# Attention stage of a transformer block: projections, value turns, reciprocals and weight splits shifted by steps, query waits by head pair

## The chip, the cores and the metric

The kernel runs on one core of a Trainium2 chip. The metric is the device time of one execution, in microseconds (us); lower is better. TensorE (PE) multiplies matrices, VectorE (DVE) and ScalarE (ACT) work elementwise and read its results from PSUM, GpSimd (POOL) works in SBUF, SyncE (SP) issues the DMAs. Each engine goes through a list of its own, and semaphores tie the lists together.

## What is computed

One block on x of shape 2 x 1024 x 512: modulated layer norm, attention, gated residual, modulated layer norm, feed-forward with ternary weights, gated residual. The change lies in the attention: 32 query heads, 8 key/value heads, 64 columns each, causal. Cut to what matters:

```python
h = _layernorm(x) * (1 + ca) + sa
q = (h @ Wq).reshape(b, s, H, D).transpose(0, 2, 1, 3)      # H = 32, D = 64
k = (h @ Wk).reshape(b, s, KVH, D).transpose(0, 2, 1, 3)    # KVH = 8
v = (h @ Wv).reshape(b, s, KVH, D).transpose(0, 2, 1, 3)
q, k = apply_rope(q, pos), apply_rope(k, pos)
k, v = jnp.repeat(k, g, axis=1), jnp.repeat(v, g, axis=1)
scores = jnp.where(causal, q @ k.T / sqrt(D), min)
attn = jax.nn.softmax(scores, axis=-1)
x = x + ga * ((attn @ v).reshape(b, s, H * D) @ Wo)
```

## The kernel before

The program has four stages one after another: `prologue` (norm, transposed input as a high and a low part), `attention`, `project_outputs`, `feed_forward`. Precision is kept by splitting each operand into a high part and a remainder: a copy in ScalarE gives the high part, a subtraction in VectorE or GpSimd the low one.

`attention` goes through eight groups, one for each key/value head with its four query heads. The order of its work is written out by hand. A group is 72 steps; every engine runs the same `step(body, T)` for T = 0 to 71 in its own list (`bodies`, L455 on; group 0 and group 7 are written out, groups 1 to 6 are a loop on each engine, and a run-in of steps 28 to 71 stands ahead of group 0, a run-out of 12 steps behind group 7). What an engine does in a step is fixed by tables:

- Each step has one tile: TensorE turns a 128x128 piece of the exponentials for four heads (`turn`, L651), ScalarE copies the high part (`high`, L695), VectorE makes the low part (`low`, L760), and TensorE multiplies both with the values two steps later (`values`, L663 and L664, `LAG` = 2). `turn(T)` also waits for the low part of T - 2.
- `rows`: a pair of query blocks takes nine steps and has eight score rows (four heads of a large block, then four of a small one), at offsets `ROW_AT` = 0, 1, 3, 4 and 5, 6, 6, 7. A row is `scores` on TensorE (L641 to L643), and one step later `maximum` on VectorE (L768) and `exponentials` on ScalarE (L708). A score writes over PSUM banks that an earlier row must have left (`ROW_FREED`: two rows before for most).
- `X_USES`: the uses of the one PSUM bank for projections, X_BANK: (kind, batch, part, start). A projection (keys and values "kv", or queries of a head pair "qx"/"qy") takes four steps on TensorE (`project`, L599 to L601, a quarter of three matmuls a step, in three steps of four beside a score row). VectorE multiplies by cosine and sine four steps after the start (`rotary_products`, L783, L784), SP swaps halves by DMA a step later (`swap`), GpSimd adds at start + 6 (L822), ScalarE copies the high part at start + 8 (L745 for queries; L741 for keys), GpSimd makes the low part (L833), and SP places both in `q_hl` at start + 10 (`place`). For "kv", ScalarE also copies the values out at start + 4 (L729).
- "v" is the turn of the values through the same bank (`turn_values`, L607), in one step; ScalarE (L734) and VectorE (L795) take the high and the low part one step later. The wait for the bank's earlier user stands at the head of the step (`await_x`).
- `D_AT` = 31 and 66: VectorE makes the reciprocals of the row sums one step ahead (L802), TensorE turns them in the same bank (`turn_den`, L619), ScalarE copies them out (L749).
- `W_HIGH` = 28 and `W_LOW` = 29: the split of the next group's weights, on ScalarE (L715 scales the key columns, L718 the high part) at the head of step 28, on VectorE (L805) at the end of step 29. There is none in group 7.

A use of the bank must find its earlier user gone:

```python
def await_x(g, n):
    uses_done.await_(pe, g, n - 1)
    if X_USES[n - 1][0] == "kv":
        kv_vt.await_(pe, g, KV.index((n - 1) % X_BODY) - (len(KV) if n == 0 else 0))
```

## Time and profile before

| what | value |
|---|---|
| median of 3 runs | 2111.36 us (2105.07 to 2113.36) |
| the profiled execution's own time | 2113.28 us |
| its span, first to last instruction | 2111.5 us |
| busy: PE, DVE, ACT, POOL | 1808.2, 1408.7, 1161.6, 796.9 us |
| mean granted clock of TensorE | 0.946 |
| first and last low part of weights (L805), in the run-in and group 6 | 89.1 and 1112.5 us |

Busy shares are averages over four stages. The distance between one group and the next, seen at L805, is (1112.5 - 89.1) / 7 = 146.2 us. In the timeline a row has the start, the time that the instruction took, and in brackets the engine's idle time before it with what ended it. TensorE's matmuls overlap, so that work is read from start to start; the idle time in brackets goes by a modelled end and comes out somewhat shorter than the gap between starts.

### The profile page before, as it was taken

To read this page: it belongs to the slowest core of one execution; us is meant where nothing else is said; L and a number is where in the kernel's file an instruction comes from. 1 tells how busy PE (TensorE), PEld (TensorE's weight loads), DVE (VectorE), ACT (ScalarE), POOL (GpSimd) and SP (SyncE) were. 2 spreads that over 40 slices of the span, in tenths; PEclk is the share of its full clock that TensorE was granted. 3 is DMA by queue.
4 is the path that set the end of the run, shared out by engine and by line. 5 is a ranking of instruction groups with operands and counts; after the bars stand their busy time and mean duration, and the time that the engine had idled before them with its cause. 6 is when DMAs were issued, how large, how long until landed. Compare 5 with 4: busy or idle time off the path is not lost. (4 is left out here: it accounts for less than half of the span.)

```text
span 2111.5 us, 30964 instructions
## 1 busy us (share of the span) xinstructions
PE 1808.2 (86%) x9601; PEld 1499.0 (71%) x9601; DVE 1408.7 (67%) x1935; ACT 1161.6 (55%) x2283; POOL 796.9 (38%) x532
## 2 busy tenths in 40 slices
PE   4679999999999999999999999357766669999997
PEld 4458878878878887787788888245555547777776
DVE  5347777767767777767777777487797946454543
ACT  1137777767767777677677678343343334232221
POOL 0023333333333333333333332175665714444443
PEclk9789999999999999999999999778888889999999
DMA  6033233233233333323332332667577510101000
GB/s 236 6 79 75 58 98 93 58 86 89 66 77 89 80 74 81 83 73 74 95 78 64 91 73 56 173 168 175 151 184 161 146 55 1 45 1 45 1 26 20
DMA packets 161113, 178.62 MB, mean 85 GB/s; under 512 B 25265, under 2 KB 112057, under 8 KB 160961
## 3 DMA queue, kind: packets, MB, share of 16 engines
q1 hardware_dynamic: 160960, 176.64, 32.9%
q8 instruction: 89, 1.46, 0.3%
q14 instruction: 64, 0.52, 0.1%
HBM read 79.83 MB, written 25.44 MB: 50 GB/s over the span
## 5 line engine op out<-in xcount | busy, mean ns | idle before, releaser
L760 DVE TENSOR_TENSOR p_lo<-ps_b,p_hi 128x512 fp32r<-128x512 f32 x576 | 396.0, 689 | 207.2 <-ACT p_hi L695 203.0
L695 ACT CAST p_hi<-ps_b 128x512 fp32r<-128x512 f32 x576 | 338.4, 587 | 253.2 <-PE ps_b L651 247.4
L768 DVE TENSOR_REDUCE negm<-ps_b 128x1 f32<-128x640 f32 (+7 forms) x512 | 379.6, 751 | 93.6 <-PE ps_b L643 89.7
L708 ACT ACTIVATE p<-ps_b,negm 128x640 f32<-128x640 f32 (+7 forms) x512 | 382.3, 749 | 67.9 <-DVE negm L768 63.3
L651 PE MATMUL ps_b<-ident,p 128*128 128x128 f32 x2304 | 352.8, 276 | 14.4 <-issue 8.7
L641 PE MATMUL ps_b<-k_hh,q_hl 128*128 128x512 f32 (+3 forms) x768 | 267.7, 349 | 16.8 <-DMA q_hl<-rot_x 12.1
L651 PEld LDWEIGHTS ps_b<-ident,p 128*128 128x128 f32 x2304 | 251.3, 141 | 41.4 <-issue 13.8
L663 PE MATMUL ps_b<-p_hi,v_hl 128*128 128x512 f32 x576 | 275.8, 479 | 1.7 <-ACT o_sb L701 1.3
L822 POOL TENSOR_TENSOR rot_c<-rot_c,rot_x 128x512 f32<-128x512 f32 (+1 forms) x96 | 123.3, 1285 | 358.1 <-DMA rot_x<-rot_s 358.1
L642 PE MATMUL ps_b<-k_l,q_hl 128*128 128x512 f32 (+3 forms) x768 | 257.0, 347 | 0.0
L977 PE MATMUL ps_c<-wo_hi,o_hi 128*128 128x512 f32 x256 | 120.4, 470 | 139.3 <-DVE o_lo L1115 139.3
L664 PE MATMUL ps_b<-p_lo,v_hl 128*128 128x512 f32 x576 | 227.9, 396 | 0.0
L817 POOL TENSOR_TENSOR o_sb<-o_sb,o_low 64x512 f32<-64x512 f32 x128 | 163.9, 1283 | 147.1 <-DMA o_low<-o_sb 147.0
L1268 PE MATMUL ps_d<-h_hi,gu 128*128 128x512 f32 x512 | 201.3, 393 | 7.8 <-ACT xn_d L1287 4.6
L1269 PE MATMUL ps_d<-h_lo,gu 128*128 128x512 f32 x512 | 200.0, 391 | 0.0
L599 PE MATMUL ps_b<-hT_hi,w_hi 128*128 128x512 f32 x384 | 157.1, 409 | 38.5 <-DVE w_lo L805 13.2
L641 PEld LDWEIGHTS ps_b<-k_hh,q_hl 128*128 128x128 f32 x768 | 145.1, 189 | 57.9 <-issue 16.9
L977 PEld LDWEIGHTS ps_c<-wo_hi,o_hi 128*128 128x128 f32 x256 | 57.9, 226 | 159.0 <-DVE o_lo L1115 90.4
L642 PEld LDWEIGHTS ps_b<-k_l,q_hl 128*128 128x128 f32 x768 | 145.4, 189 | 28.0
L600 PE MATMUL ps_b<-hT_hi,w_lo 128*128 128x512 f32 x384 | 153.6, 400 | 0.0
L601 PE MATMUL ps_b<-hT_lo,w_hi 128*128 128x512 f32 x384 | 152.2, 396 | 0.0
L1436 DVE TENSOR_TENSOR a<-ps_d,sg 128x512 f32<-128x512 f32 x64 | 44.2, 691 | 158.5 <-PE ps_d L1269 140.8
(141 smaller groups left out, 3420.9 us busy)
## 6 DMA issues: line engine op xcount, KB each, us to landing
rot_x<-rot_s SPq DMA_DIRECT2D x320, 64.0 KB, 2.0
q_hl<-rot_s SPq DMA_DIRECT2D x128, 128.0 KB, 2.3
q_hl<-rot_x SPq DMA_DIRECT2D x128, 128.0 KB, 2.4
o_low<-o_sb SPq DMA_DIRECT2D x128, 128.0 KB, 2.2
attention_out<-o_sb SPq DMA_DIRECT2D x128, 128.0 KB, 2.5
o_raw<-attention_out SPq DMA_DIRECT2D x32, 512.0 KB, 4.9
rd<-attention_out SPq DMA_DIRECT2D x64, 256.0 KB, 9.0
wf<-in_L_ffn_w_gate_up SPq DMA_DIRECT2D x16, 512.0 KB, 11.6
```

Source lines behind the costliest of these rows:

```text
L641: pe.matmul(ps[:, bank, 0:n], q, k_hh[:, unit, k0:k0 + n], start=True, stop=False)
L642: ins = pe.matmul(ps[:, bank, 0:n], q, k_l0[:, unit, k0:k0 + n], start=False, stop=(k0 + n < nk))
L651: ins = pe.transpose(ps[:, T_BANK + T % 2, h * P:(h + 1) * P], p_32[:, parity, h, column * P:(column + 1) * P], ident[:])
L663: pe.matmul(ps[:, O_BANK, :], v_hl[:, unit, j, :], p_hi[:, T % P_RING, :], start=(j == 0), stop=False)
L664: pe.matmul(ps[:, O_BANK, :], v_hl[:, unit, j, :], p_lo[:, T % P_RING, :], start=False, stop=(j == i)).then_inc(pv_done, 1)
L695: act.copy(p_hi[:, T % P_RING, :], ps[:, T_BANK + T % 2, :]).then_inc(phi_ready, 1)
L708: act.activation(p_32[:, parity, h, column * P:column * P + nk], s, ACT.Exp, bias=negm[:, k:k + 1], scale=1.0, accum_out=den[:, unit, h, i ...
L760: dve.tensor_tensor(p_lo[:, T % P_RING, :], ps[:, T_BANK + T % 2, :], p_hi[:, T % P_RING, :].bitcast(F32), ALU.subtract).then_inc(plo_read ...
L768: dve.tensor_reduce(negm[:, k:k + 1], s, AX.X, ALU.max, negate=True).then_inc(max_ready, 1)
L977: pe.matmul(ps[:, i, t, :], hi, wo_hi[:, kk, :], start=(kk == 0), stop=False)
L1268: pe.matmul(ps[:, bank + half, :], gu[:, m, half, k, :], h_hi[:, parity, k, :], start=(k == 0), stop=False)
L1269: i = pe.matmul(ps[:, bank + half, :], gu[:, m, half, k, :], h_lo[:, parity, k, :], start=False, stop=(k == CT - 1))
```

## The change

Four things. In `X_USES` the four query projections of batch 1 start one step later (9, 14, 19, 24 become 10, 15, 20, 25), with all that hangs on them by an offset, on every engine and in SP's queue; the turn of batch 0's values starts one step earlier (44 becomes 43), with its copies. The weight split moves one step later on both engines (28, 29 become 29, 30). The reciprocals move one step earlier on VectorE, to two steps ahead of their turn. And TensorE's wait for placed queries, which stood ahead of the first row of a block for both head pairs, is divided: ahead of row 0 for the first pair, and ahead of row 2, the first to read the second pair's heads, for the second.

```diff
--- before.py
+++ after.py
@@ -290,15 +290,15 @@
 RB = PAIRS * len(ROWS)
 ROWS_BEFORE = 8
 
-X_USES = [("kv", 1, 1, 1), ("v", 1, 0, 7), ("qx", 1, 0, 9), ("qx", 1, 1, 14), ("qy", 1, 0, 19), ("qy", 1, 1, 24),
-          ("kv", 0, 0, 33), ("kv", 0, 1, 38), ("v", 0, 0, 44), ("qx", 0, 0, 46), ("qx", 0, 1, 51), ("qy", 0, 0, 56),
+X_USES = [("kv", 1, 1, 1), ("v", 1, 0, 7), ("qx", 1, 0, 10), ("qx", 1, 1, 15), ("qy", 1, 0, 20), ("qy", 1, 1, 25),
+          ("kv", 0, 0, 33), ("kv", 0, 1, 38), ("v", 0, 0, 43), ("qx", 0, 0, 46), ("qx", 0, 1, 51), ("qy", 0, 0, 56),
           ("qy", 0, 1, 61), ("kv", 1, 0, 68)]
 X_HERE = 6
 LAST_ROW = {("qx", 0): 39, ("qy", 0): 55, ("qx", 1): 7, ("qy", 1): 23}
 X_BODY = len(X_USES)
 D_AT = [31, 66]
 START = 28
-W_HIGH, W_LOW, W_LOAD = 28, 29, 2
+W_HIGH, W_LOW, W_LOAD = 29, 30, 2
 
 
 class Events:
@@ -622,16 +622,17 @@
                 unit, _, i, h, _, k = row_of(r)
                 first = (r // 8 + 1) % 4
                 if k == 0 and first == 0:
-                    for n in ([7, 9, 10] if unit == 0 else [0, 2, 3]):
-                        if X_USES[n][0] == "kv":
-                            kv_lo.await_(pe, g, KV.index(n))
-                            kv_hi.await_(pe, g, KV.index(n))
-                        else:
-                            q_place[buf_of(n)].await_(pe, g, QBUF[buf_of(n)].index(n))
-                if k == 0 and first == 2:
-                    for n in ([11, 12] if unit == 0 else [4, 5]):
-                        buf = buf_of(n)
-                        q_place[buf].await_(pe, g, QBUF[buf].index(n) - (len(QBUF[buf]) if unit == 0 else 0))
+                    n = 7 if unit == 0 else 0
+                    kv_lo.await_(pe, g, KV.index(n))
+                    kv_hi.await_(pe, g, KV.index(n))
+                if k in (0, 2) and first == 0:
+                    n = (9 if unit == 0 else 2) + h // 2
+                    buf = buf_of(n)
+                    q_place[buf].await_(pe, g, QBUF[buf].index(n))
+                if k in (0, 2) and first == 2:
+                    n = (11 if unit == 0 else 4) + h // 2
+                    buf = buf_of(n)
+                    q_place[buf].await_(pe, g, QBUF[buf].index(n) - (len(QBUF[buf]) if unit == 0 else 0))
                 rows_p.await_(pe, g, r - ROW_FREED[k])
                 nk = (i + 1) * P
                 q = q_hl[:, h, i * P:(i + 1) * P]
@@ -796,7 +797,7 @@
                                       v_hl[:, unit, :, 0:D].bitcast(F32), ALU.subtract).then_inc(x_used, 1)
                 for g, t in body.tile(T, 0):
                     low(g, t)
-                for g, d in body.dens(T, -1):
+                for g, d in body.dens(T, -2):
                     rows_p.await_(dve, g, 23 if d == 0 else 55)
                     dens_turned.await_(dve, g, d - 1)
                     dve.reciprocal(rd[:], den[:, d].rearrange("p h i -> p (h i)")).then_inc(rd_ready, 1)
```

In the changed kernel, lines behind the waits are numbered one higher (L805 is L806). Where the program moves, in the loop of groups 1 to 6; rows that only set registers and wait for nothing are left out.

VectorE, steps 28 to 31, before (b_whi_ready is the high weights' semaphore, b_phi_ready that of a tile's high part, b_s_ready that of a score row):

```order
L783 TENSOR_TENSOR rot_c<-ps_b,cos 128x512 [waits b_x_ready]
L784 TENSOR_TENSOR rot_s<-ps_b,sin 128x512
L768 TENSOR_REDUCE negm<-ps_b 128x1 [waits b_s_ready]
L760 TENSOR_TENSOR p_lo<-ps_b,p_hi 128x512 [waits b_phi_ready]
L768 TENSOR_REDUCE negm<-ps_b 128x1 [waits b_s_ready]
L760 TENSOR_TENSOR p_lo<-ps_b,p_hi 128x512 [waits b_phi_ready]
L805 TENSOR_TENSOR w_lo<-w_raw,w_hi 128x1536 [waits b_whi_ready]
L760 TENSOR_TENSOR p_lo<-ps_b,p_hi 128x512 [waits b_phi_ready]
L802 RECIPROCAL rd_b<-den 128x32 [waits b_rd_turned,b_p_ready]
L768 TENSOR_REDUCE negm<-ps_b 128x1 [waits b_s_ready]
```

and now:

```order
L784 TENSOR_TENSOR rot_c<-ps_b,cos 128x512 [waits b_x_ready]
L785 TENSOR_TENSOR rot_s<-ps_b,sin 128x512
L769 TENSOR_REDUCE negm<-ps_b 128x1 [waits b_s_ready]
L761 TENSOR_TENSOR p_lo<-ps_b,p_hi 128x512 [waits b_phi_ready]
L803 RECIPROCAL rd_b<-den 128x32 [waits b_rd_turned,b_p_ready]
L761 TENSOR_TENSOR p_lo<-ps_b,p_hi 128x512 [waits b_phi_ready]
L806 TENSOR_TENSOR w_lo<-w_raw,w_hi 128x1536 [waits b_whi_ready]
L769 TENSOR_REDUCE negm<-ps_b 128x1 [waits b_s_ready]
L761 TENSOR_TENSOR p_lo<-ps_b,p_hi 128x512 [waits b_phi_ready]
```

The rotation (cosine, sine) stands behind step 28's low part and not ahead of its maximum; the reciprocal has come forward by one low part; the low part of the weights stands behind step 30's low part and directly ahead of a maximum.

ScalarE, steps 27 to 30, before (rot_s is a query copy, b_t_ready the turn's semaphore):

```order
L745 CAST rot_s<-rot_c 128x512 [waits b_rotated0]
L715 ACTIVATE w_raw<-w_raw 128x4x64 [waits b_w_in]
L316 REGISTER_ALU [waits b_k_scaled]
L718 CAST w_hi<-w_raw 128x1536 [waits b_x_ready]
L695 CAST p_hi<-ps_b 128x512 [waits b_pv_done,b_t_ready]
L701 COPY o_sb<-ps_b 128x512 [waits b_o_out1,b_pv_done]
L708 ACTIVATE p,den<-ps_b,negm 128x1024 [waits b_max_ready]
L695 CAST p_hi<-ps_b 128x512 [waits b_pv_done,b_t_ready]
```

and now:

```order
L696 CAST p_hi<-ps_b 128x512 [waits b_pv_done,b_t_ready]
L702 COPY o_sb<-ps_b 128x512 [waits b_o_out1,b_pv_done]
L709 ACTIVATE p,den<-ps_b,negm 128x1024 [waits b_max_ready]
L746 CAST rot_s<-rot_c 128x512 [waits b_rotated0]
L716 ACTIVATE w_raw<-w_raw 128x4x64 [waits b_w_in]
L316 REGISTER_ALU [waits b_k_scaled]
L719 CAST w_hi<-w_raw 128x1536 [waits b_x_ready]
L696 CAST p_hi<-ps_b 128x512 [waits b_pv_done,b_t_ready]
L709 ACTIVATE p,den<-ps_b,negm 128x1024 [waits b_max_ready]
```

The query copy, the scaling and the high weights stand behind a high copy, an output copy and an exponential row that they stood ahead of.

TensorE, steps 43 and 44, before (b_x_used and b_vt_ready are the semaphores of the bank's earlier user):

```order
L663 MATMUL ps_b<-p_hi,v_hl 128x512 [waits b_plo_ready]
L664 MATMUL ps_b<-p_lo,v_hl 128x512
L641 MATMUL ps_b<-k_hh,q_hl 128x256 [waits b_p_ready]
L642 MATMUL ps_b<-k_l,q_hl 128x256
L643 MATMUL ps_b<-ident_r,mask_r 128x128
L316 REGISTER_ALU [waits b_x_used]
L316 REGISTER_ALU [waits b_p_ready,b_vt_ready]
L651 MATMUL ps_b<-ident,p 128x128 [waits b_plo_ready]
L651 MATMUL ps_b<-ident,p 128x128 x3
L663 MATMUL ps_b<-p_hi,v_hl 128x512 [waits b_plo_ready]
L664 MATMUL ps_b<-p_lo,v_hl 128x512
L607 MATMUL ps_b<-ident,rot_c 128x64 x8
```

and now:

```order
L316 REGISTER_ALU [waits b_x_used]
L316 REGISTER_ALU [waits b_vt_ready]
L652 MATMUL ps_b<-ident,p 128x128 [waits b_plo_ready]
L652 MATMUL ps_b<-ident,p 128x128 x3
L664 MATMUL ps_b<-p_hi,v_hl 128x512 [waits b_plo_ready]
L665 MATMUL ps_b<-p_lo,v_hl 128x512
L607 MATMUL ps_b<-ident,rot_c 128x64 x8
L642 MATMUL ps_b<-k_hh,q_hl 128x256 [waits b_p_ready]
L643 MATMUL ps_b<-k_l,q_hl 128x256
L644 MATMUL ps_b<-ident_r,mask_r 128x128
L316 REGISTER_ALU [waits b_p_ready]
L652 MATMUL ps_b<-ident,p 128x128 [waits b_plo_ready]
```

The wait for b_x_used and b_vt_ready now stands ahead of step 43's turn, and the value turn (L607) ahead of step 43's score.

## Rows read from the trace of the kernel before

**Rows 1.** The page's part on engines: busy us (share of the span) xinstructions

```profile
PE 1808.2 (86%) x9601; PEld 1499.0 (71%) x9601; DVE 1408.7 (67%) x1935; ACT 1161.6 (55%) x2283; POOL 796.9 (38%) x532
```

**Rows 2.** Who waited for whom, TensorE: us in total, times, longest

```profile
PE ps_b L619 <- DVE rd_b L802: 13.9, 15, 1.3
...
PE ps_b L641 <- DMA q_hl<-rot_x: 12.1, 8, 2.8
PE ps_b L599 <- DVE v_hl L795: 11.1, 16, 1.4
```

**Rows 3.** Timeline, group 3, steps 8 to 10, VectorE then TensorE

```profile
615.90 1.28 DVE L760 TENSOR_TENSOR p_lo<-ps_b,p_hi 128x512 fp32r<-128x512 f32 x2
...
616.04 0.50 PE L599 MATMUL ps_b<-hT_hi,w_hi 128*128 128x512 f32 x1 [0.97 <-DVE v_hl L795]
...
617.60 0.61 PE L651 MATMUL ps_b<-ident,p 128*128 128x128 f32 x4
```

**Rows 4.** Timeline, group 3, steps 27 to 32: TensorE, ScalarE, VectorE

```profile
652.76 0.40 PE L599 MATMUL ps_b<-hT_hi,w_hi 128*128 128x512 f32 x1
...
653.46 0.40 PE L641 MATMUL ps_b<-k_hh,q_hl 128*128 128x512 f32 x1
...
654.43 0.60 PE L651 MATMUL ps_b<-ident,p 128*128 128x128 f32 x4
...
663.68 0.33 PE L641 MATMUL ps_b<-k_hh,q_hl 128*128 128x128 f32 x1
...
652.98 0.62 ACT L745 CAST rot_s<-rot_c 128x512 fp32r<-128x512 f32 x1
...
655.41 0.58 ACT L695 CAST p_hi<-ps_b 128x512 fp32r<-128x512 f32 x1
...
657.46 0.60 ACT L695 CAST p_hi<-ps_b 128x512 fp32r<-128x512 f32 x1
...
659.03 1.31 ACT L695 CAST p_hi<-ps_b 128x512 fp32r<-128x512 f32 x2
662.42 1.12 ACT L708 ACTIVATE p<-ps_b,negm 128x1024 f32<-128x1024 f32 x1 [2.09 <-DVE negm L768]
...
658.09 0.69 DVE L760 TENSOR_TENSOR p_lo<-ps_b,p_hi 128x512 fp32r<-128x512 f32 x1 [0.23 <-ACT p_hi L695]
...
661.22 1.16 DVE L768 TENSOR_REDUCE negm<-ps_b 128x1 f32<-128x1024 f32 x1
```

**Rows 5.** Timeline, group 3, steps 43 to 46: TensorE, ScalarE, VectorE

```profile
685.14 0.62 PE L651 MATMUL ps_b<-ident,p 128*128 128x128 f32 x4
...
687.09 0.65 PE L651 MATMUL ps_b<-ident,p 128*128 128x128 f32 x4 [0.56 <-ACT rot_c L729]
...
691.86 0.50 PE L599 MATMUL ps_b<-hT_hi,w_hi 128*128 128x512 f32 x1 [0.28 <-DVE v_hl L795]
...
686.38 0.58 ACT L729 COPY rot_c<-ps_b 64x512 f32<-64x512 f32 x1
...
691.12 0.69 DVE L795 TENSOR_TENSOR v_hl<-ps_b,v_hl 128x512 fp32r<-128x512 f32 x1 [1.42 <-ACT v_hl L734]
```

**Rows 6.** Timeline, group 3, steps 63 to 68: TensorE, then ScalarE

```profile
728.22 0.49 PE L641 MATMUL ps_b<-k_hh,q_hl 128*128 128x512 f32 x1 [1.10 <-DMA q_hl<-rot_x]
...
739.31 0.22 PE L641 MATMUL ps_b<-k_hh,q_hl 128*128 128x128 f32 x1
...
733.69 1.11 ACT L708 ACTIVATE p<-ps_b,negm 128x1024 f32<-128x1024 f32 x1 [0.57 <-DVE negm L768]
...
737.30 1.12 ACT L708 ACTIVATE p<-ps_b,negm 128x1024 f32<-128x1024 f32 x1 [0.23 <-DVE negm L768]
```

**Rows 7.** Timeline and one stretch (busy by engine, then PEclk): group starts, group 6

```profile
595.03 1.05 PE L651 MATMUL ps_b<-ident,p 128*128 128x128 f32 x4 [1.86 <-issue]
...
595.14:598.55 3.41, 3.41 (x13) 3.03 (x14) 0.69 (x1) 1.17 (x2) 0.34 (x1) 0.50 0.45 112
...
1182.98 0.49 PE L641 MATMUL ps_b<-k_hh,q_hl 128*128 128x512 f32 x1 [2.12 <-DMA q_hl<-rot_x]
```

## The prediction

> **What bounds the kernel now.** The share of busy time comes first: TensorE 86%, VectorE 67%, ScalarE 55% [rows 1]. The change touches only the attention stage, so the next view is who TensorE waits for. Of its waits there, three kinds belong to instructions that the change moves: 13.9 us for the reciprocals, 12.1 us for placed queries (the longest, 2.8 us, in the run-in before the first group), 11.1 us for split values [rows 2]. That is 37.1 us, under 2% of the time. For the rest of the stage TensorE's queue is the clock: eight groups of 72 steps. Then I read the timeline of one ordinary group (group 3 of 0 to 7) around each moved instruction, on TensorE, ScalarE and VectorE side by side. Each of these works strictly through its own list, so the question at every place is not who is late now, but what stands next in line when a stall goes. Times below are starts unless I say otherwise; I sum against the profiled execution (span 2111.5, own time 2113.28 us) and carry the difference over to the median of 2111.36.
>
> **Query projections of batch 1 one step later (9 to 10, and so on).** At step 9 TensorE stands still until the values' low half is made, and projects at 616.04 [rows 3]. With the projection at step 10, that wait is covered by step 9's scores. But the same VectorE queue makes step 8's low part after the low values, at 615.90, for 0.69 us, so until 616.65 with the signal; and TensorE's turn of step 10 must have it. Before, that turn stood at 617.60 with a projection quarter of about 0.70 us (652.76 to 653.46) done that is now still to do [rows 3, 4]. Gain: 617.60 - 616.65 - 0.70 = 0.25 us a group, not the 1 us of the stall: 8 x 0.25 = -2.0 us. The later multiplications on VectorE, copies on ScalarE and GpSimd, and the swap and place DMAs of SP all move by the same step; their readers stand five steps or more behind, so no queue there gets late.
>
> **Steps 27 to 32: the weight split and the first reciprocal.** This is the largest term. ScalarE has 2.43 us of work (query copy 652.98, then key scaling and high weights, until 655.41) which now comes one step later [rows 4]. Before, it sat where ScalarE had nothing else; step 28's high copy followed at 655.41 and step 29's at 657.46, 2.05 us on. Now step 28's high copy comes first. The turn that it reads stands at 654.43 before; the projection quarter of step 24 has moved behind it, so it comes 0.70 earlier, at 653.73, and the copy some 0.64 later, 654.37. Then the 2.05 us, and then the 2.43 us: step 29's high copy is at 654.37 + 2.05 + 2.43 = 658.85, 1.39 later than before. VectorE's low part of step 29 follows by 0.63, at 659.48 against 658.09 [rows 4]. From there to the maximum of the third wide row VectorE has 3.13 us of work in both orders (661.22 - 658.09: two low parts, low weights, reciprocal). But the low weights now stand behind step 30's low part, which waits for ScalarE: high copy 30 at 658.85 + 1.57 = 660.42, so 661.05 for the low part, while VectorE is free at 660.35. That adds 0.70. The maximum comes at 661.22 + 1.39 + 0.70 = 663.31. Exponential (1.20 on) and the score that waits for it (1.26 on) follow: 665.77 against 663.68 [rows 4]. The stall on the reciprocal goes entirely, and is already inside this difference: TensorE waits for the exponential in its place. That is 2.09; with a few hundredths for each signal that has no row of its own I take **+2.2 us for the seven groups** that split weights, +15.4 us. Bounds: 0, if ScalarE drains faster than its rows say, to 2.5 (x7 = 17.5). The last group has no split: 0.
>
> **Value turn one step earlier (44 to 43).** The wait for the previous projection's user stands at the head of the step. ScalarE's copy of the values starts at 686.38, and TensorE resumes at 687.09 [rows 5]. That copy depends on nothing in step 43, so its time stays; TensorE now stops at 685.14 and not after step 43. The stall grows from 0.72 (1.95 less 1.23 us of work in step 43) to 1.95. In return the 0.45 us before the projection at 691.86 (0.28 by the ends of the matmuls) is covered: +0.78 net if nothing else is late. Something is: the low values (691.12) now stand ahead of step 44's low part, as at step 8, and TensorE's turn 46 needs that part. ScalarE reaches the high values at about the same time as before, so that part ends at 691.12 + 0.60 + 0.69 = 692.41, the turn is at 692.48 instead of 690.49, and the projection 0.92 later at 693.40: +1.54. I take **+1.5 x 7 = +10.5 us**, with +0.8 and +1.6 as ends, since the low part's place in the queue is fixed by the order.
>
> **Waits divided by head pair, second reciprocal.** At step 63 the first score waits for a placement that only the third one, at step 66, reads. This goes: 1.26 us here (728.22; 1.10 in the row by the ends), 9.3 us by ends over the seven groups, 10.4 us by starts [rows 2, 6]. At step 66 the stall on the reciprocal goes too, but the chain VectorE to ScalarE to VectorE takes over: with the reciprocal at step 64, ahead of the rotation, the exponential of 733.69 comes 1.26 - 0.26 = 1.00 earlier, and so does that at 737.30; the score that needs it comes 1.26 us after, at 737.56 against 739.31. So 1.75 us where the placement stall was 1.26: 0.5 more. Sum: 10.4 + 7 x 0.5 = **-13.9 us**. In the run-in the 2.8 us stall goes [rows 2]: -2.8 us. The waits at steps 9, 27 and 45 do not bind now.
>
> **Clock.** The new idle times, 1.95 us at step 43 and some 2.4 us at step 32, are as long as some at the group's start. One of those, 1.86 us, was followed by a stretch granted 0.50, that is 1.2 GHz instead of 2.4 [rows 7]; it cost that group some 1.6 us (half of 3.4). I allow one or two such stretches, +2 us; the bounds are 0 and all fourteen new idle times, +22 us.
>
> Sum: -2.0 + 15.4 + 10.5 - 13.9 - 2.8 + 2 = **+9 us**: 2120 on the median. Half a percent, 10.6 us, is about what can be told from no change here: faster is under 2101, slower over 2122.
>
> **A rule against this.** TensorE has the highest occupancy [rows 1], and VectorE and ScalarE have a third or more of their time free. The Trainium skill (Perfetto Trace Analysis, section Identifying the Most-Contended Engine) says that the engine with the highest occupancy is the one to optimise first. By that rule work shifted on the other two is free and the stalls taken from TensorE are the result: the first rival. The rows of steps 28 to 30, where ScalarE and VectorE have next to no gaps, speak against it.
>
> **Rivals.** (1) *All three kinds of stall vanish and nothing else is late*: -37.1 us, 2074. For it: each stall has a named releaser that the change moves away. Against: at steps 8 and 29 the next instruction in the same queues is read by TensorE within two steps. Chance 0.08. (2) *The pile-up at 28 to 32 does not cost*, because ScalarE and VectorE recover before TensorE needs the third wide row, and the turn at 43 costs only 0.8: -2.0 + 0 + 5.6 - 13.9 - 2.8 = -13, 2098. It needs ScalarE to gain 2 us in three steps in which it has no gap. Chance 0.15. (3) *Slower, by the clock*: the long new idles are followed by the 1.2 GHz level in most groups. Each costs 1.6 us; with seven or more of the fourteen it is +7 + 11 to +22, 2129 to 2140, so 2134. It decides from about three stretches on. For it: 1.86 us was enough once. Against: the stall before 1182.98 in another group, which was longer, was not followed by it; the matmul after it took 0.49 us, as at 728.22 [rows 6, 7]. Chance 0.20. (4) Forecast: 2120, its own range 2112 to 2128, chance 0.57.
>
> **Range and chances.** 2098 to 2135 leaves out rival 1, half of rival 2 and the upper part of rival 3, under 0.2. Faster: rival 1 and two thirds of rival 2, 0.18. Slower: rival 3 and the upper part of the forecast's range, 0.42. Same: 0.40. The forecast lies just under the bound.
>
> **What would show it.** In the profile after: TensorE's wait for split values before the projection gone, and waits for low parts (turn 10, turn 31, turn 46) in its place; no wait for reciprocals in groups with a split, but a wait for the exponential of about 2.5 us at step 32; the wait for the value copy about 1.9 instead of 0.6 us; no wait for placed queries; a wait for an exponential near step 68. A wait for the low parts that stays under 0.3 us at turns 31 and 46 would refute the two large terms; the count of stretches at 0.50 settles the clock.

## The result, and the profile after

The changed kernel takes 2136.36 us (median of 6 runs, 2132.55 to 2149.44) where the kernel before takes 2110.86 us beside it (6 runs, 2105.07 to 2113.57): a ratio of **1.0133, 95% interval 1.0102 to 1.0163**. It is slower by 25.5 us. The forecast was 2120, its range 2098 to 2135: the sign of the sum was right, its size was not, and the time lies just above the range.

The profiled execution had its own time of 2149.44 us, a span of 2147.6 us and a mean granted clock of 0.936. It is the longest of the six. A second profiled execution of the same kernel (below) had a span of 2134.5; where one number might depend on the execution I give both.

The page's part on engines, after (the line that answers to [rows 1]): busy us (share of the span) xinstructions.

```profile
PE 1838.7 (86%) x9601; PEld 1529.7 (71%) x9601; DVE 1409.6 (66%) x1935; ACT 1158.0 (54%) x2283; POOL 791.6 (37%) x532
```

The number of instructions is the same on each engine. VectorE, ScalarE and GpSimd are busy for the same time within 6 us; TensorE is busy 30.5 us longer (1838.7 against 1808.2) with the same 9601 matmuls. More busy time for equal work is the first sign that the clock has a part in this.

Who waited for whom on TensorE, after: us in total, times, longest. It answers to [rows 2].

```profile
PE ps_b L642 <- ACT p L709: 28.8, 27, 3.3
PE ps_b L652 <- DVE p_lo L761: 16.7, 20, 1.0
...
PE ps_b L652 <- issue: 12.5, 6, 2.4
PE ps_b L652 <- ACT rot_c L730: 10.6, 6, 1.8
```

Of the rows of the attention stage, scores that wait for an exponential (L642, L709), turns that wait for a low part (L652, L761), and turns of step 43, which now stand behind the value turn's wait for the copy of the values (L730), have grown most. The reciprocal and the placed queries, 13.9 and 12.1 us in [rows 2], have no row left, and the wait for split values (11.1 us there) has shrunk to 1.4 us, once. So nearly 36 us of stalls that the change was to remove are gone, and three rows have 56 us of waits where the kernel before had 9 us in them (4.3, 0.9 and 3.9).

A table by stretches of a group says where the time went. Each number is the time from the turn (matmul L651, after L652) of one step to that of another, from starts in the timeline of TensorE. "Before" is group 3; "after" is group 3 of the first execution, which happened to have no stretch at 1.2 GHz at steps 31 to 48; the last column is what the other groups of that execution showed.

| steps of a group | before | after, group 3 | after, other groups with the split |
|---|---|---|---|
| 9 to 14 | 11.62 | 11.38 | 11.37 to 11.39 |
| 14 to 27 | 26.25 | 25.62 | 25.62 |
| 27 to 33 | 12.21 | 15.62 | 15.46 to 15.88 |
| 33 to 36 | 5.98 | 5.77 | 7.34 to 8.36 |
| 38 to 43 | 10.87 | 12.77 | 12.77 to 12.84 |
| 43 to 48 | 9.89 | 9.69 | 9.66 to 9.69, or 11.71 to 11.73 |
| 63 to 69 | 14.23 (mean of seven 14.44) | 12.39 | 12.38 to 12.39 |

**Steps 27 to 32.** Timeline, after, group 3: ScalarE, VectorE, GpSimd, TensorE. It answers to [rows 4].

```profile
670.31 0.59 ACT L696 CAST p_hi<-ps_b 128x512 fp32r<-128x512 f32 x1 [1.80 <-PE ps_b L652]
...
672.38 0.63 ACT L746 CAST rot_s<-rot_c 128x512 fp32r<-128x512 f32 x1
...
673.43 1.48 ACT L719 CAST w_hi<-w_raw 128x1536 fp32r<-128x1536 f32 x1
674.81 0.58 ACT L696 CAST p_hi<-ps_b 128x512 fp32r<-128x512 f32 x1
...
681.07 1.11 ACT L709 ACTIVATE p<-ps_b,negm 128x1024 f32<-128x1024 f32 x1 [3.61 <-DVE negm L769]
...
675.42 0.69 DVE L761 TENSOR_TENSOR p_lo<-ps_b,p_hi 128x512 fp32r<-128x512 f32 x1 [1.40 <-ACT p_hi L696]
...
677.00 0.69 DVE L761 TENSOR_TENSOR p_lo<-ps_b,p_hi 128x512 fp32r<-128x512 f32 x1 [0.63 <-ACT p_hi L696]
677.61 2.29 DVE L806 TENSOR_TENSOR w_lo<-w_raw,w_hi 128x1536 fp32r<-128x1536 f32 x1
679.82 1.21 DVE L769 TENSOR_REDUCE negm<-ps_b 128x1 f32<-128x1024 f32 x1
...
676.99 1.30 POOL L823 TENSOR_TENSOR rot_c<-rot_c,rot_x 128x512 f32<-128x512 f32 x1 [1.30 <-DMA rot_x<-rot_s]
...
676.16 0.66 PE L652 MATMUL ps_b<-ident,p 128*128 128x128 f32 x4 [0.94 <-DVE p_lo L761]
...
682.32 0.33 PE L642 MATMUL ps_b<-k_hh,q_hl 128*128 128x128 f32 x1 [3.03 <-ACT p L709]
```

Read it from the top: step 28's high copy (670.31), then the query copy and the high weights, and only then step 29's high copy at 674.81. VectorE's low part of step 29 follows at 675.42. The low weights (L806, 677.61) stand behind step 30's low part, and the maximum that the exponential needs comes at 679.82, the exponential at 681.07, the score at 682.32. This is the predicted chain, link for link. One link has another length: the low weights take 2.29 us; in the kernel before they take 1.75 (the experiments below say why). The score stood still for 3.03 us, where I had said about 2.5.

**Steps 43 to 46.** Timeline, after, group 3: ScalarE, VectorE, TensorE. It answers to [rows 5].

```profile
704.80 0.58 ACT L730 COPY rot_c<-ps_b 64x512 f32<-64x512 f32 x1
...
709.82 0.69 DVE L796 TENSOR_TENSOR v_hl<-ps_b,v_hl 128x512 fp32r<-128x512 f32 x1 [1.59 <-ACT v_hl L735]
710.42 1.28 DVE L761 TENSOR_TENSOR p_lo<-ps_b,p_hi 128x512 fp32r<-128x512 f32 x2
...
705.51 0.65 PE L652 MATMUL ps_b<-ident,p 128*128 128x128 f32 x4 [1.77 <-ACT rot_c L730]
...
711.16 0.66 PE L652 MATMUL ps_b<-ident,p 128*128 128x128 f32 x4 [0.82 <-DVE p_lo L761]
...
712.12 0.39 PE L599 MATMUL ps_b<-hT_hi,w_hi 128*128 128x512 f32 x1
```

The turn of step 43 stands idle for 1.77 us by the ends of the matmuls (0.56 in [rows 5]), because the value turn's wait is now at the head of that step. The projection at 712.12 waits for nothing; in its place the turn of step 46, at 711.16, waits 0.82 us for a low part that is behind the low values.

**Steps 63 to 68.** Timeline, after, group 3: TensorE and ScalarE. It answers to [rows 6].

```profile
757.53 0.33 PE L642 MATMUL ps_b<-k_hh,q_hl 128*128 128x128 f32 x1 [0.27 <-ACT p L709]
...
752.70 1.12 ACT L709 ACTIVATE p<-ps_b,negm 128x1024 f32<-128x1024 f32 x1 [0.77 <-DVE negm L769]
...
756.27 1.11 ACT L709 ACTIVATE p<-ps_b,negm 128x1024 f32<-128x1024 f32 x1 [1.27 <-DVE negm L769]
```

The score follows its exponential (756.27) after 1.26 us, as predicted, and is idle for only 0.27 us.

**The clock.** Timeline of TensorE, after, group 2, at steps 32 and 43, and then busy time by engine in four stretches (us, PE busy (x), PEld busy (x), DVE, ACT and POOL busy (x), PEclk, DMA share, GB/s). The first three windows follow step 43 of group 2, step 32 of group 2 and step 32 of group 4; the last one follows step 43 of group 3.

```profile
525.60 0.33 PE L642 MATMUL ps_b<-k_hh,q_hl 128*128 128x128 f32 x1 [2.99 <-ACT p L709]
...
550.37 0.65 PE L652 MATMUL ps_b<-ident,p 128*128 128x128 f32 x4 [1.77 <-ACT rot_c L730]
```

```profile
551.00:557.80 6.80, 6.80 (x29) 5.34 (x28) 2.77 (x5) 4.21 (x11) 1.04 (x1) 0.50 0.00 1
527.10:530.50 3.40, 3.40 (x14) 3.04 (x14) 1.27 (x3) 2.19 (x8) 1.27 (x1) 0.50 0.19 42
837.70:841.10 3.40, 3.40 (x13) 2.92 (x12) 1.58 (x3) 3.04 (x7) 0.16 (x1) 0.50 0.05 10
...
705.50:712.30 6.80, 5.97 (x41) 5.00 (x42) 3.79 (x7) 4.46 (x12) 1.28 (x1) 1.00 0.06 14
```

After the idle of 2.99 us at step 32 and after that of 1.77 us at step 43 there are 3.4 and 6.8 us at a granted clock of 0.50, the 1.2 GHz level. In 6.8 us at 0.50 TensorE did 29 matmuls, at 1.00 it did 41. In the seven groups with a split, ten of the fourteen places are followed by such a stretch: step 32 in groups 0, 1, 2, 4, 5 and 6, step 43 in groups 1, 2, 5 and 6. A stretch after step 32 makes steps 33 to 36 take 7.35 us instead of 5.77, one after step 43 makes steps 43 to 48 take 11.7 instead of 9.69. In all: 6 x 1.58, and 1.0 more in group 1, whose stretch is longer (6.8 us), is 10.5; 4 x 2.02 is 8.1; together **18.6 us**. (The 6.8 us behind step 43 cost less than half their length; the 0.82 us that the turn of step 46 waits in group 3 is not there in these groups, so a part of the slow work falls into that wait.)

The account of the attention stage, from its first to its last matmul (1234.0 us before, 1265.6 after, by these profiled executions):

| term | predicted | found in the trace | from |
|---|---|---|---|
| query projections, step 9 to 14 | -2.0 | -1.9 | 8 x (11.38 - 11.62) |
| steps 14 to 36 without the clock | +15.4 | +18.0 | 7 x (47.01 - 44.44), group 3 |
| value turn, steps 38 to 48 without the clock | +10.5 | +11.9 | 7 x (22.46 - 20.76) |
| waits divided and second reciprocal, 63 to 69 | -13.9 | -14.4 | 7 x (12.39 - 14.44) |
| run-in to the first group | -2.8 | -2.9 | 51.79 against 54.70 |
| clock | +2 | +18.6 | the paragraph above |
| sum | +9 | +29.3 | measured +31.5; the loop's head (step 69 to 0) has most of the rest, 2.1 |

### The profile page after: what moved, and what is told of

It reads as the page before. It is cut to its first block and busy times, and to the rows that moved or that the text cites. A ratio compares the mean times of both kernels' runs of the same rounds, so it can differ in the third digit from the quotient of the medians.

```text
span 2147.6 us, 30941 instructions
## 1 busy us (share of the span) xinstructions
PE 1838.7 (86%) x9601; PEld 1529.7 (71%) x9601; DVE 1409.6 (66%) x1935; ACT 1158.0 (54%) x2283; POOL 791.6 (37%) x532
## 5 line engine op out<-in xcount | busy, mean ns | idle before, releaser
L761 DVE TENSOR_TENSOR p_lo<-ps_b,p_hi 128x512 fp32r<-128x512 f32 x576 | 395.1, 688 | 227.2 <-ACT p_hi L696 222.4
L709 ACT ACTIVATE p<-ps_b,negm 128x640 f32<-128x640 f32 (+7 forms) x512 | 382.6, 750 | 76.5 <-DVE negm L769 72.1
L652 PE MATMUL ps_b<-ident,p 128*128 128x128 f32 x2304 | 360.2, 280 | 40.8 <-DVE p_lo L761 16.7
L652 PEld LDWEIGHTS ps_b<-ident,p 128*128 128x128 f32 x2304 | 256.5, 143 | 72.9 <-DVE p_lo L761 32.9
L642 PE MATMUL ps_b<-k_hh,q_hl 128*128 128x512 f32 (+3 forms) x768 | 270.6, 352 | 29.0 <-ACT p L709 28.8
L664 PE MATMUL ps_b<-p_hi,v_hl 128*128 128x512 f32 x576 | 280.3, 487 | 1.1 <-ACT o_sb L702 0.6
L823 POOL TENSOR_TENSOR rot_c<-rot_c,rot_x 128x512 f32<-128x512 f32 (+1 forms) x96 | 123.5, 1286 | 393.3 <-DMA rot_x<-rot_s 393.3
L642 PEld LDWEIGHTS ps_b<-k_hh,q_hl 128*128 128x128 f32 x768 | 148.0, 193 | 71.6 <-ACT p L709 37.0
L599 PE MATMUL ps_b<-hT_hi,w_hi 128*128 128x512 f32 x384 | 156.6, 408 | 28.7 <-DVE w_lo L806 13.2
L601 PE MATMUL ps_b<-hT_lo,w_hi 128*128 128x512 f32 x384 | 153.4, 399 | 0.0
```

The source lines that it names most:

```text
L642: pe.matmul(ps[:, bank, 0:n], q, k_hh[:, unit, k0:k0 + n], start=True, stop=False)
L652: ins = pe.transpose(ps[:, T_BANK + T % 2, h * P:(h + 1) * P], p_32[:, parity, h, column * P:(column + 1) * P], ident[:])
L664: pe.matmul(ps[:, O_BANK, :], v_hl[:, unit, j, :], p_hi[:, T % P_RING, :], start=(j == 0), stop=False)
L709: act.activation(p_32[:, parity, h, column * P:column * P + nk], s, ACT.Exp, bias=negm[:, k:k + 1], scale=1.0, accum_out=den[:, unit, h, i ...
L761: dve.tensor_tensor(p_lo[:, T % P_RING, :], ps[:, T_BANK + T % 2, :], p_hi[:, T % P_RING, :].bitcast(F32), ALU.subtract).then_inc(plo_read ...
```

## The experiments

All differences below are edits of the kernel before or of the changed kernel. The kernel before ran beside each of them: 2113.31 us (23 runs) beside the waits alone, the value turn alone, projections with split, and the useless work; 2112.78 (7 runs) beside the query projections alone, the sum that waits, the waits with reciprocals, and the low weights in two parts; 2113.94 (10 runs) beside the other three. Each ratio is to these.

### The three parts of the change, one by one

**The waits alone**, on the kernel before:

```diff
-                    for n in ([7, 9, 10] if unit == 0 else [0, 2, 3]):
...
+                if k in (0, 2) and first == 0:
+                    n = (9 if unit == 0 else 2) + h // 2
+                    buf = buf_of(n)
+                    q_place[buf].await_(pe, g, QBUF[buf].index(n))
```

> The kernel before with the waits for queries divided by head pair, and nothing else. Queue theory: the stall ahead of step 63's first score goes in seven groups (10.4 us by starts) and in the run-in (2.8 us); the reciprocal still stands behind step 65's low part, so the chain VectorE to ScalarE moves by just the stall and nothing comes on top: 2111 - 13 = 2098 us. Rival: the placement is merely awaited three steps later, at step 66, and the stall reappears there: 2111 us, with a wait for placed queries of about 1 us ahead of the third row. Clock: no new idle time, so no more stretches at 0.50 in the attention stage than the two of before.

Measured: 2097.34 us (9 runs, 2090.95 to 2107.71), ratio 0.9919 (0.9893 to 0.9944). The wait for placed queries has no row any more, so the rival (the stall comes back at step 66) is refuted, and steps 63 to 69 take 12.88 us (12.77 in group 0). This part gains 16 us by itself. I had priced it at 10.4 and 2.8, that is 13.2; the ratio's interval, 12 to 23 us, holds that.

**The value turn alone** at step 43, on the kernel before:

```diff
-          ("kv", 0, 0, 33), ("kv", 0, 1, 38), ("v", 0, 0, 44), ("qx", 0, 0, 46), ("qx", 0, 1, 51), ("qy", 0, 0, 56),
+          ("kv", 0, 0, 33), ("kv", 0, 1, 38), ("v", 0, 0, 43), ("qx", 0, 0, 46), ("qx", 0, 1, 51), ("qy", 0, 0, 56),
```

> The kernel before with the turn of batch 0's values at step 43 instead of 44, and nothing else. Queue theory: the wait for the value copy grows from 0.6 to about 1.8 us, the wait ahead of step 46's projection goes and one for step 44's low part takes its place: 1.7 us for each of seven groups, +12 us. Clock theory: the idle time is followed by a stretch at 0.50 in about four of the seven groups, 2 us each, +8 us: 2131 us. Without the clock's part: 2123 us. If the loss seen in the changed kernel came only because it was late from step 33 already: no change, 2111 us.

Measured: 2132.05 us (9 runs, 2129.67 to 2148.61), ratio 1.0084 (1.0057 to 1.0111). Steps 38 to 43 take 12.78 to 12.86 us in the groups with a split (10.87 before); the wait L651 for the copy is 10.6 us, 6 times, longest 1.8, just as in the changed kernel. Three of the seven groups (2, 4 and 6) have a stretch at 0.50 after it. The median is where I had expected it (2131), but not all of it for the reason that I gave: these stretches cost 3.9 us by steps 43 to 48 (10.53, 11.70 and 10.76 instead of 9.67 to 9.69), not 8. Another 4.8 us lie at steps 63 to 69, where two groups (1 and 2) have a stretch at 0.50 behind the wait for placed queries; that wait is 1.3 to 2.1 us in groups 1 to 6. So half of the clock's share was hit by luck.

**Query projections and weight split together**, without the divided waits and with the old reciprocal:

```diff
-X_USES = [("kv", 1, 1, 1), ("v", 1, 0, 7), ("qx", 1, 0, 9), ("qx", 1, 1, 14), ("qy", 1, 0, 19), ("qy", 1, 1, 24),
+X_USES = [("kv", 1, 1, 1), ("v", 1, 0, 7), ("qx", 1, 0, 10), ("qx", 1, 1, 15), ("qy", 1, 0, 20), ("qy", 1, 1, 25),
...
-W_HIGH, W_LOW, W_LOAD = 28, 29, 2
+W_HIGH, W_LOW, W_LOAD = 29, 30, 2
```

> The kernel before with the four query projections one step later and the weight split at steps 29 and 30, and nothing else (reciprocals at their old place). Queue theory: 0.24 us gained at step 9 in eight groups, some 2.7 us lost from step 27 to step 33 in seven, because the high weights stand ahead of step 29's high copy and the low weights behind step 30's low part: +17 us. Clock theory on top: the idle time at step 32 is followed by a stretch granted 0.50 in most groups, 1.4 to 1.6 us each, +9 us: 2137 us together. If the clock has nothing to do with it: 2128 us and no stretches at 0.50 after step 32. Rival (the low weights are slowed by the GpSimd sum beside them, not by their place in the queue): the low weights take 2.1 us or more here too, and the rest of the loss is small.

Measured: 2141.55 us (4 runs, 2139.43 to 2155.91), ratio 1.0138 (1.0087 to 1.0189). Steps 27 to 33 take 16.6 to 17.4 us, over one more than in the changed kernel. The waits of TensorE say why (us in total, times, longest):

```profile
PE ps_b L641 <- DMA q_hl<-rot_x: 22.1, 16, 2.8
PE ps_b L641 <- ACT p L708: 17.5, 18, 2.0
```

The wait for placed queries comes 16 times instead of 8 [rows 2]. The scores of step 27 wait for the first two query projections of batch 1, one for each head pair, at once. The second of them now starts at step 15 and is placed at step 25, which is late for step 27: the score stands still for 0.92 us in group 3 (at 660.91), and the row has grown by 10 us for eight groups. The prediction said that the waits at step 27 do not bind; that holds in the kernel before, and it holds in the changed kernel only because that one has divided them. So two parts of the change lean on each other here. The 2137 us that I had expected did not have this wait. The rival, low weights slowed to 2.1 us or more by GpSimd's sum, is refuted as the cause of this loss: they take 1.86 to 1.92 us here. The idle time at step 32 is 1.8 to 2.0 us, and in four of the seven groups (1, 3, 5 and 6) a stretch at 0.50 follows it.

Added up by ratios, the three parts give -0.81 + 0.84 + 1.38 = +1.41%, and the whole is +1.33%. That is agreement within the intervals only (0.3, 0.3 and 0.5), which together leave room for over 10 us. By the attention stages of the profiled executions the three give -13.5 + 21.5 + 30.3 = +38 us and the whole +31.5 (+29.7 in its second execution): the 10 us of waits at step 27 are counted in the parts and do not exist in the whole.

**Query projections alone**, the split left at steps 28 and 29 (only the first of the two edits above):

> The kernel before with the four query projections one step later, and nothing else: the weight split stays at steps 28 and 29. ScalarE then waits at the head of step 28 for a projection that TensorE makes in that step. Queue theory, worked out from the rows of the kernel before: step 29's high copy comes about 2.1 us later than before, the third wide maximum about 2.5 us later; less than with the split moved as well (4.2 to 4.6 us there, with the reciprocal at its old place). So 2111 - 2 + 17 = 2126 us, and up to 8 us more where stretches at 0.50 follow: 2126 to 2134. Rival (the split has to move with the projections, and its own move costs nothing): the same as with both moved, 2141 us, or slower.

Measured: 2158.13 us (4 runs, 2149.89 to 2162.54), ratio 1.0206 (1.0174 to 1.0239). This expectation (2126 to 2134) was wrong in direction: I had thought that the split, left where it was, would cost less. It costs some 15 us more than both together; the rival, the same as with both moved or slower, is what came. Some of the 15 us are the clock's: all seven groups have a stretch at 0.50 at steps 31 to 32, where the run with both has four. Timeline, group 3: ScalarE, VectorE, GpSimd, TensorE.

```profile
664.75 0.42 ACT L715 ACTIVATE w_raw<-w_raw 128x256 f32<-128x256 f32 x1
669.39 1.48 ACT L718 CAST w_hi<-w_raw 128x1536 fp32r<-128x1536 f32 x1 [4.22 <-PE ps_b L601]
670.77 0.57 ACT L695 CAST p_hi<-ps_b 128x512 fp32r<-128x512 f32 x1
...
674.91 2.83 DVE L805 TENSOR_TENSOR w_lo<-w_raw,w_hi 128x1536 fp32r<-128x1536 f32 x1
...
674.85 1.28 POOL L817 TENSOR_TENSOR o_sb<-o_sb,o_low 64x512 f32<-64x512 f32 x1
677.23 1.64 POOL L822 TENSOR_TENSOR rot_c<-rot_c,rot_x 128x512 f32<-128x512 f32 x1 [1.10 <-DMA rot_x<-rot_s]
...
678.73 0.28 PE L619 MATMUL ps_b<-ident,rd_b 128*32 128x128 f32 x1 [2.56 <-DVE rd_b L802]
```

The new high weights overwrite those that the last query projection still reads. They stand at the head of step 28 in ScalarE's list, and that projection now ends in the same step: they wait 4.22 us for its last matmul (L601), and step 28's high copy (670.77) stands behind them. Moving the split along by a step was therefore the better choice once the projections had moved. The 18 us of steps 14 to 36 in the changed kernel are thus a price of moving the projections with the split behind them, which lands where ScalarE and VectorE are already late. What the split costs when it moves alone was not measured.

### The low weights of 2.1 to 2.6 us

In the changed kernel the low weights took 2.20, 2.14, 2.25, 2.29, 2.14, 2.29 and 2.58 us in groups 0 to 6, beside GpSimd's sum (L823) for 0.58, 0.53, 0.63, 0.68, 0.52, 0.68 and 0.96 us. In the kernel before, beside nothing, they took 1.75 in every group. In the timeline of steps 27 to 32 above the sum starts at 676.99 and ends at 678.29, the low weights at 677.61. So GpSimd's sum was made to wait for them:

```diff
                     buf_swap[buf].await_(pool, g, BUF[buf].index(n))
+                    if n == X_HERE - 1 and body.holds(0, 0, KVH - 2):
+                        splits_lo.await_(pool, g, 0)
```

> The changed kernel, in which GpSimd's sum for the last query projection of batch 1 waits until the low weights are made (seven groups), so that the two do not lie side by side. In the changed kernel the low weights take 2.14 to 2.58 us where a sum of GpSimd overlaps them, 1.75 in the kernel before where none does. Theory (VectorE's operation with two inputs in SBUF waits for GpSimd's): the low weights are back at 1.75 us, the score at step 32 stands 0.4 to 0.8 us earlier, some 3.5 us in all and a little more if a stretch at 0.50 goes: 2132 us against the 2136 of the changed kernel. Rival: the low weights are slower because of something else at that place (ScalarE's copies, DMAs): 2.1 us or more as before, and no gain.

Measured: 2132.15 us (4 runs, 2128.0 to 2137.69), ratio 1.0087 (1.0059 to 1.0114). Timeline of VectorE and GpSimd, group 3:

```profile
668.05 1.75 DVE L806 TENSOR_TENSOR w_lo<-w_raw,w_hi 128x1536 fp32r<-128x1536 f32 x1
...
669.88 1.26 POOL L825 TENSOR_TENSOR rot_c<-rot_c,rot_x 128x512 f32<-128x512 f32 x1 [3.75 <-DVE w_lo L806]
```

With nothing beside them they take 1.75 us again, in all groups, and steps 27 to 33 take 15.01 to 15.09 us instead of 15.46 to 15.88: 7 x 0.56 = 3.9 us by the trace. The median is 4.2 us lower; by the ratios it is more (0.46%, 9.7 us), but eight stretches at 0.50 follow the two steps instead of ten (groups 2, 3, 5 and 6 at both), so I take the trace's 4 us as the size. The rival, something else at that place, is refuted. This is the part by which the second term was too small: 18.0 - 4.0 = 14.0 against the 15.4 predicted.

Each overlap lengthens the low weights by nearly the whole overlap (0.54 us for 0.68, in the run with the query projections alone 1.08 for 1.22), and there the operation of GpSimd that began *while* the low weights ran (677.23) took 1.64 us instead of 1.28. The one that comes second is held up. The run with useless work below has both cases as well: in groups 2 to 5 GpSimd's sum begins 0.07 to 0.24 us behind the low weights, which take 1.75 us, and the sum takes 2.65 to 2.83 us instead of 1.29; in groups 1 and 6 it begins ahead of them, and they take 2.84 and 2.78 us. The Trainium skill (SBUF — State Buffer, section Who interferes with whom) says that a VectorE instruction with two inputs in SBUF contends with a GpSimd instruction that reads SBUF, and that the issue order decides who blocks; the trace agrees both ways round.

### The clock, with useless work in the idle time

In every group with a split, TensorE does 16 useless transposes ahead of the value turn's wait at step 43 and 8 useless matmuls ahead of the late score of step 32. The results of the kernel are the same; the work is extra.

```diff
+            def fill_turns(g, T):
...
+                for _ in range(4):
+                    for h in range(GQ):
+                        pe.transpose(ps[:, T_BANK + T % 2, h * P:(h + 1) * P],
+                                     p_32[:, parity, h, column * P:(column + 1) * P], ident[:])
+            def fill_bank(g):
+                for _ in range(8):
+                    pe.matmul(ps[:, O_BANK, :], k_l0[D:P, 1, 0:P], k_hh[D:P, 1, 0:512], start=False, stop=False)
```

> The changed kernel with useless matmuls put into TensorE's two new idle times: 16 transposes ahead of the wait at step 43 (a bank that the next turn writes over) and 8 matmuls with zeros ahead of the score at step 32. They take 1.4 and 1.9 us of idle times of 1.95 and about 2.9 us. Clock theory: TensorE now does more work and ends earlier, since the stretches at 0.50 after steps 32 and 43 (10 in the profile of the changed kernel) do not come: some 18 us less than the profiled run of the changed kernel, 8 to 12 us less than its median of 2136, so 2124 to 2128 us. Queue theory alone (the clock follows something else): the fillings lie in idle time and cost nothing, 2136 us, and as many stretches at 0.50 as without them.

Measured: 2130.45 us (10 runs, 2118.86 to 2134.76), ratio 1.0063 (1.0038 to 1.0088), span 2117.1. That is over the 2124 to 2128 expected and under the 2136 of the rival; the count of stretches decides between them. Timeline of TensorE in group 2 at step 43, then at step 32, and the stretch behind step 43 that answers to the one from 551.00 above:

```profile
535.35 1.93 PE L661 MATMUL ps_b<-ident,p 128*128 128x128 f32 x16
537.21 0.66 PE L652 MATMUL ps_b<-ident,p 128*128 128x128 f32 x4
```

```profile
511.54 2.10 PE L666 MATMUL ps_b<-k_hh,k_l 64*128 64x512 f32 x8
514.10 0.33 PE L642 MATMUL ps_b<-k_hh,q_hl 128*128 128x128 f32 x1 [0.46 <-ACT p L726]
```

```profile
537.20:544.00 6.80, 5.97 (x42) 5.00 (x42) 3.88 (x7) 4.47 (x12) 1.27 (x1) 1.00 0.06 14
```

The kernel with more work is the faster one. Steps 38 to 43 last nearly as long as before the filling (12.70 us, before 12.8), so nothing of the stall itself is won; but no stretch at 0.50 follows step 43 in any group and only one follows step 32 (group 1), and outside that group steps 33 to 36 take 5.77 us, and 43 to 48 take 9.66 to 9.70 in all. The attention stage is 19.5 us shorter than in the first execution of the changed kernel and 17.7 shorter than in the second. (Not all of that is the clock: in groups 2 to 5 the low weights begin ahead of GpSimd's sum and take 1.75 us, which is 2 us in all; in groups 1 and 6 they take longer, and steps 27 to 33 with them, so that 1 us is left.) By the times the gain is smaller: 8.4 us by the differences to the kernel before beside each (17.1 against 25.5), 15 by the ratios. The profiled execution was the fastest of its ten, so others may have had more such stretches than it. The clock term is thus 8 to 18 us, on any count several times the 2 that I had put.

The Trainium skill (TensorE: Matmul & The Clock Gate, section What's actually happening) says that the lower level is the default and that activity releases it. The trace agrees: ten stretches at 0.50 without the useless matmuls, one with them.

### The same kernel again, and the value turn back in its place

**Again**, unaltered:

> The changed kernel, unaltered, for a second profiled execution. In the first one ten stretches at a granted clock of 0.50 followed the new idle times (six after step 32, four after step 43), and that execution was 13 us above the kernel's own median. If the clock term is made by those stretches, a second execution near the median should have fewer or shorter of them: about 10.4 + 8.1 - 13 = some 5 to 6 us instead of 18.5 in the groups, that is three to five of the fourteen places, and steps 27 to 33 and 38 to 43 unchanged within 0.1 us (15.46 to 15.88, 12.8). If instead the stretches are a fixed part of this order of work, ten again, and the spread between executions lies outside the attention stage. Median 2136 either way.

Measured: 2138.26 us (4 runs, 2132.0 to 2147.09), ratio 1.0128 (1.0091 to 1.0165); the profiled execution has a span of 2134.5. I had expected three to five stretches after steps 32 and 43 in it. There are ten, as in the first one, at other places: step 32 in groups 0, 1, 2, 3, 4 and 6, step 43 in groups 1, 2, 3 and 4. Two of them:

```profile
543.00:549.80 6.80, 6.80 (x30) 5.54 (x29) 2.04 (x4) 3.62 (x10) 1.27 (x1) 0.50 0.02 4
519.10:522.50 3.40, 3.40 (x14) 3.02 (x13) 1.67 (x5) 2.41 (x7) 0.91 (x1) 0.51 0.19 43
```

The attention stage is nearly as long (1263.7 against 1265.6 us), so the rival that I had named holds: ten of fourteen belong to this order of work, and 11 of the 13 us between the two executions lie elsewhere. The turn of step 0 in group 0 starts at 146.17 us in the first execution and at 138.49 in the second: 7.7 of the 13.1 us have come together before the first group begins, and 7.0 of them before the attention stage's first matmul (94.4 against 87.3 us), in a part of the program that the change does not touch. The executions of the other kernels fall on 138 to 147 us at this place as well, the kernel before on 145.73. The cause is open.

**The changed kernel with the value turn back at step 44:**

```diff
-          ("kv", 0, 0, 33), ("kv", 0, 1, 38), ("v", 0, 0, 43), ("qx", 0, 0, 46), ("qx", 0, 1, 51), ("qy", 0, 0, 56),
+          ("kv", 0, 0, 33), ("kv", 0, 1, 38), ("v", 0, 0, 44), ("qx", 0, 0, 46), ("qx", 0, 1, 51), ("qy", 0, 0, 56),
```

> The changed kernel with the value turn back at step 44; nothing else differs. By my terms the turn costs 7 x 1.7 = 12 us without the clock and the low stretches behind step 43 another 0 to 8: 2136 - 12 - (0 to 8) = 2116 to 2124, centre 2120. Steps 38 to 43 should come back to 10.87 us from 12.8, 43 to 48 to 9.9, and no stretch at 0.50 should follow step 43; those after step 32 stay. The rival, that the value turn costs little in this order because the pile-up at 27 to 33 leaves the same queues late anyway: 2132 to 2136.

Measured: 2124.7 us (7 runs, 2119.11 to 2129.91), ratio 1.0047 (1.0024 to 1.0069): 13.6 us under the changed kernel beside it, just over the upper edge of what was expected (2116 to 2124); the rival, 2132 to 2136, is refuted. By the profiled executions the attention stage is 1245.1 us, 18.6 less than the second one of the changed kernel, against 20 from 11.9 for the queue and 8.1 for the clock, less 1.6 for one more stretch after step 32. Steps 38 to 43 are back at 10.84 to 10.93 us, and no stretch at 0.50 follows step 43; step 32 is followed by one in all seven groups. So the value turn's term is confirmed from both sides: added to the kernel before and taken from the changed one.

### Towards a faster version

**Divided waits and the reciprocal two steps ahead**, all else as before:

```diff
-                for g, d in body.dens(T, -1):
+                for g, d in body.dens(T, -2):
```

> The kernel before with the divided waits and the reciprocals two steps ahead. Queue theory: step 63 to 69 comes down from 12.88 us (waits alone) to 12.39 in seven groups, 3.5 us, since the reciprocal leaves the place behind step 65's low part; at step 31 the wait for the reciprocal goes and one for the exponential at step 32 takes its place, with no gain, because VectorE does the same work up to the third wide maximum. Together 2097 - 3.5 = 2094 us. Rival (the wait for the reciprocal at step 31, 1.26 us, is time of its own): 9 us more, 2085 us.

Measured: 2098.32 us (4 runs, 2089.69 to 2104.45), ratio 0.9938 (0.9915 to 0.996). Steps 63 to 69 go from 12.88 to 12.39 us, the 0.5 a group that the prediction had given the second reciprocal; steps 27 to 33 stay at 12.19, since the wait of the reciprocal is taken over by that of an exponential. Only the profile tells it from the waits alone; the times (2097.34 there, and 2094 expected here) do not.

**The low weights in two parts** on top of that: those that the next key and value projection needs (512 columns) at step 29, the other 1024 at step 35, and the wait of the value turn behind the turn of its step.

```diff
-W_HIGH, W_LOW, W_LOAD = 28, 29, 2
+W_HIGH, W_LOW, W_LATE, W_LOAD = 28, 29, 35, 2
...
-                for g, n, _ in body.uses(T, 0, kinds=("v",)):
-                    await_x(g, n)
                 for g, t in body.tile(T, 0):
                     turn(g, t)
+                for g, n, _ in body.uses(T, 0, kinds=("v",)):
+                    await_x(g, n)
```

> The kernel before with the divided waits and early reciprocals, and two changes of mine at the places that the study points to: the low weights in two parts (the key and value columns at step 29, 0.7 us, the query columns at step 35, 1.2 us, first read at step 46), and TensorE's wait ahead of a value turn placed behind the step's own turn of exponentials. Queue theory: the third wide maximum comes 1.05 us earlier in seven groups, so 7.4 us on top of the waits and reciprocals; the late wait covers 0.36 us at step 44 in seven groups, 2.5 us, and 0.28 at step 7 in eight, 2 us, of which the low values ahead of the projection at steps 9 and 46 may take a part back: 2094 - 7 - 2 = 2085 us. Rival (VectorE is not what step 32 waits for): no gain over the waits and reciprocals, 2094 us.

Measured: 2093.7 us (4 runs, 2084.44 to 2095.49), ratio 0.9892 (0.9863 to 0.992). Steps 27 to 33 take 11.31 us (12.19 before the edit), but steps 38 to 43 take 11.0 to 11.95 (10.87), which gives about two thirds of it back (4.0 of 6.2 us over seven groups). I had expected 2085 us. The number is that of the rival, 2094, but its reason is refuted: step 32 does come earlier. Timeline of TensorE, group 3, at step 38:

```profile
664.00 0.50 PE L602 MATMUL ps_b<-hT_hi,w_hi 128*128 128x512 f32 x1 [1.26 <-ACT rot_c L733]
```

**The second part at step 39**, where VectorE has gaps:

```diff
-W_HIGH, W_LOW, W_LATE, W_LOAD = 28, 29, 35, 2
+W_HIGH, W_LOW, W_LATE, W_LOAD = 28, 29, 39, 2
```

> The candidate with the second part of the low weights at step 39 instead of 35. In the candidate steps 38 to 43 take 11.0 to 11.95 us where the kernel before takes 10.87. Theory: the second part (about 1.1 us of VectorE) makes the maximum of step 35's row late, so the exponential waits 0.65 us, the copy of the rotated values stands behind it in ScalarE, and the projection of step 38 waits 1.26 us instead of 0.63. At step 39 VectorE has gaps of 0.78, 0.79 and 0.71 us, so 38 to 43 should be 10.9 to 11.2, and the wait for that copy 0.6 instead of 1.26: 7 x 0.4 = 3 us less, 2091. Rival: the later wait of the value turn makes the difference; then 38 to 43 stays at 11.5 on average and the time at 2094.

Measured: **2084.68 us** (4 runs, 2081.33 to 2088.19), ratio **0.9862** (0.9838 to 0.9886), the fastest version here: 29 us under the kernel before, 54 under the changed one, and 6 under the 2091 that I had expected. The same place in the timeline, the row of that wait over the whole program, and the form of the low weights (duration in ns min/median/max, first and last start):

```profile
662.06 0.50 PE L602 MATMUL ps_b<-hT_hi,w_hi 128*128 128x512 f32 x1 [0.60 <-ACT rot_c L733]
```

```profile
PE ps_b L602 <- ACT rot_c L733: 4.3, 7, 0.7
```

```profile
L810 DVE TENSOR_TENSOR w_lo<-w_raw,w_hi x8: 628/629/693, 90.3 to 1090.9; 128x512 fp32r<-128x512 f32 x8
L813 DVE TENSOR_TENSOR w_lo<-w_raw,w_hi x8: 1207/1220/1280, 97.4 to 1109.7; 128x1024 fp32r<-128x1024 f32 x8
```

The wait is 0.60 us again (8.4 us in all with the second part at step 35, 4.3 here), and steps 38 to 43 take 10.85 to 10.86 (10.95 in group 0). The theory holds in its chain: at step 35 the second part had made a maximum late, behind it an exponential, behind that the copy that the projection waits for. But the place in the queue is the smaller half of it. In groups 2 to 6 the second part at step 35 falls beside a sum of GpSimd that began before it, and takes 1.71 to 2.20 us; there steps 38 to 43 take 11.47 to 11.95. Group 3 of that run:

```profile
657.05 1.28 POOL L825 TENSOR_TENSOR o_sb<-o_sb,o_low 64x512 f32<-64x512 f32 x1 [2.46 <-DMA o_low<-o_sb]
...
657.71 1.71 DVE L813 TENSOR_TENSOR w_lo<-w_raw,w_hi 128x1024 fp32r<-128x1024 f32 x1
```

In groups 0 and 1 it takes 1.24 and 1.22 us, and they take 11.08 and 11.01. At step 39 it takes 1.21 to 1.28 us in all groups. So most of the loss was the overlap with GpSimd once more. The rival, the moved wait of the value turn, is refuted, for it is in both kernels. The trace gives 7 x 0.6 for the edit; the medians differ by 9, and the two were not run beside each other. Against the waits alone, which give 16 of the 29 us by themselves, the reciprocal (0.5 a group), the divided low weights (0.9 a group at steps 27 to 33) and, by its place, the later wait of the value turn (0.3 at steps 0 to 9, 0.2 at 43 to 48; not run by itself) are worth some 13 by the rows.

## Why the prediction was off, step by step

**Query projections at step 9: right.** -2.0 predicted, -1.9 found. Timeline of TensorE, after, group 3, the turn of step 10:

```profile
632.74 0.65 PE L652 MATMUL ps_b<-ident,p 128*128 128x128 f32 x4 [0.82 <-DVE p_lo L761]
```

It waits 0.82 us for a low part where the projection had waited 0.97 for the values [rows 3]: one stall exchanged for another, and a quarter of a microsecond left over.

**Steps 27 to 32: mechanism right, 2.6 us too small, and over the upper bound of 17.5.** The order of late instructions (step 29's high copy, low part 30, low weights, maximum, exponential, score) is what the trace shows. The step that failed here is "VectorE has 3.13 us of work in both orders": one of those pieces, the low weights, grew from 1.75 to 2.29 us because in the new order it falls beside GpSimd's sum. The run in which the sum waits shows this to be worth 4 us; without it the term is 14.0.

**Value turn: mechanism right, 1.4 us too small.** +10.5 predicted, +11.9 in the trace (1.7 a group, where the upper end was 1.6), and +18.7 by the times of the run with the value turn alone, with what the clock adds. Both halves were seen, the idle at the head of step 43 (1.95 by starts) and the exchange of the projection's wait for the turn's. The prediction left the low values where they were; they come 5.02 us after the start of the copy of the values (704.80 to 709.82) instead of 4.74 (686.38 to 691.12 in [rows 5]).

**Waits, second reciprocal, run-in: right.** -13.9 and -2.8 predicted, -14.4 and -2.9 found. "The waits at steps 9, 27 and 45 do not bind now" would have been wrong at step 27 for the query projections without the divided waits, as the run of the two edits alone shows.

**Clock: this is the step that failed.** "I allow one or two such stretches, +2 us". There were ten of fourteen, in each of two executions, worth 18.6 us in the trace and 8 to 18 by the runs. The bounds, 0 to 22, held it; the value taken between them did not. I had taken it from one idle that was followed by a slow stretch and one that was not, both at other places of the group, and had weighed the second, harmless one as if it were half of all the evidence. The trace of the kernel before has one more that I did not use, at the head of group 5 (timeline, then one stretch):

```profile
898.06 0.65 PE L651 MATMUL ps_b<-ident,p 128*128 128x128 f32 x4 [2.07 <-issue]
```

```profile
898.95:902.35 3.40, 3.40 (x12) 2.94 (x12) 1.78 (x2) 1.54 (x3) 0.73 (x1) 0.50 0.33 83
```

So two of its three idle times over 1.8 us between the starts of group 0 and of group 7 were followed by such a stretch. Two thirds of fourteen places at 1.6 us each are an estimate of 15 us, where I had put 2. The third rival named this mechanism, with seven or more of fourteen and 2129 to 2140 us: that is what happened, at a chance of 0.20. That the sign came out right is in part luck, for +9 us was less than the 10.6 us that can be told from no change. Without the clock the terms come to +10.7 us, where the prediction had +7: that would have been inside the forecast's own range.

**The rule against.** The Trainium skill (Perfetto Trace Analysis, section Identifying the Most-Contended Engine) says to optimise the engine with the highest occupancy first. As I had read it, work shifted on the less busy engines would be free. The trace does not bear that reading out: for 36 us of removed stalls TensorE has 47 us of new waits (56 less the 9 of before), for engines that are a third or more of the time free [rows 1], since each of them works through its list in order.

## What to carry to other kernels

When an instruction is moved in a queue that is worked through in order, ask for the next reader behind it, not for the stall that goes: here each removed stall came back as another, except where a wait was made narrower (divided by head pair) or work was cut so that only what is needed soon stands in the busy place. When a change makes TensorE idle in one piece for about two microseconds, once in each pass of a loop, price the slow clock that may follow for half of the passes or more, not for one or two. And look at what a moved VectorE operation with two inputs in SBUF will run beside on GpSimd.

## What the runs showed of the hardware

An idle of 1.77 us at step 43 was followed by 6.8 us at 1.2 GHz in four of seven groups, and one of some 3.0 us at step 32 by 3.4 us (6.8 in group 1) in six of seven, in two executions of the same kernel at different groups. With the value turn alone moved the same 1.77 us had 3.4 or 6.8 us of it in three of seven. At steps 31 and 32 the other kernels show it in four of seven groups after 1.8 to 2.0 us (projections with split), in four of seven after 2.5 us (the sum that waits), in seven of seven at 2.4 to 2.6 us (projections alone) and in seven of seven at 2.9 to 3.3 us (value turn back). In a few of these groups the stretch began within the idle time. Groups with and without the slow stretch do not differ in the length of the idle (in group 3 of the first execution 3.03 and 1.77 us were followed by none), so the length of one idle does not decide it; what does is left open. Useless matmuls in the idle time made the kernel faster, although they took nothing off the wait itself. And an overlap of GpSimd's sum with the low weights on VectorE lengthened the one that began second by nearly the overlap: on VectorE 0.54 us for 0.68 and 1.08 for 1.22, on GpSimd from 1.29 to 2.83 us where the sum began 0.07 us behind the low weights.
